# Soft mixture and rotary step: one product split over two engines, one maximum moved, one step spread over three engines

## The reference

```python
logits = einsum('bmd,dnp->bmnp', x, phi)        # 16 batches, 256 tokens, 64 x 32 slots
D = softmax(logits, over the batches)
C = softmax(logits, over all slots)
slots = einsum('bmd,bmnp->bnpd', x, D)
y = einsum('bmnp,bnpd->bmd', C, slots @ W + b)
```

```python
q, k = rms_norm(q), rms_norm(k)                 # over the 8 values of a head
q, k = apply_rope(q, cos, sin) * q_gain, apply_rope(k, cos, sin)
k = repeat(k, 4, heads)
```

## Time and profile before

| what | us |
|---|---|
| median of three runs | 3475.13 |
| lowest and highest | 3470.81, 3478.71 |
| the profiled execution, its own time | 3474.84 |
| its span in the trace | 3473.0 |
| TensorE busy in the span | 2850.8 (82%) |
| VectorE busy | 2255.4 (65%) |
| ScalarE busy | 1846.9 (53%) |
| GpSimd busy | 473.9 (14%) |
| chain that ended last | TensorE 54%, VectorE 33%, ScalarE 9% |

### The profile page before, as it was taken

How to read it: one execution, slowest core, us unless ns; L and a number is a source line. 1 busy time by engine, 2 the same in 40 slices (tenths; PEclk the granted TensorE clock), 3 DMA queues, 4 the chain that set the end, 5 groups by cost and what they waited for, 6 DMA issues and landing times.

```text
span 3473.0 us, 75794 instructions
## 1 busy us (share of the span) xinstructions
PE 2850.8 (82%) x31896; PEld 2280.3 (66%) x31896; DVE 2255.4 (65%) x5958; ACT 1846.9 (53%) x4107; POOL 473.9 (14%) x535
## 2 busy tenths in 40 slices
PE   5788887788888578788886889988888899686895
PEld 3566665556666477777775767866767688575474
DVE  4766656676666588888896754466575644754527
ACT  3566665566666477777774444354544434443332
POOL 1211101210001232222221011110000211002000
PEclk8899999999999889998998899997999999797897
DMA  2000000000000000000001000010010000001000
GB/s 94 1 2 2 1 2 1 1 2 1 14 2 14 28 7 7 7 7 7 7 1 61 3 2 25 2 50 2 17 36 3 25 2 26 26 3 49 0 1 25
DMA packets 16996, 48.95 MB, mean 14 GB/s; under 512 B 1168, under 2 KB 9616, under 8 KB 14096
## 3 DMA queue, kind: packets, MB, share of 16 engines
q1 hardware_dynamic: 16656, 44.10, 3.7%
HBM read 41.99 MB, written 2.10 MB: 13 GB/s over the span
## 4 chain that ended last, share of the span: by engine, by line
PE 54%; DVE 33%; ACT 9%; issue 2%; POOL 1%; DMA 0%; DVEq 0%; SPq 0%; POOLq 0%; ACTq 0%
PE ps L329 7%; DVE LN L2048 5%; PE ps L320 5%; PE ps L1926 3%; PE ps L1357 3%; PE ps L386 3%; PE ps L473 3%; DVE M L489 2%; DVE RS L239 2%; DVE LN L2061 2%; PE ps L1368 2%; PE ps L294 2%; PE ps L1870 2%; PE ps L754 2%; ACT LN L302 1%
## 5 line engine op out<-in xcount | busy, mean ns | idle before, releaser
L302 ACT COPY LN<-ps 128x512 f32<-128x512 f32 (+4 forms) x560 | 286.3, 550 | 277.5 <-PE ps L294 55.2
L281 POOL TENSOR_TENSOR RS<-RS,MISC 128x4 f32<-128x4 f32 x184 | 189.1, 1028 | 1462.7 <-DVE RS L263 781.1
L489 DVE TENSOR_REDUCE M<-ps 128x6 f32<-128x768 f32 x256 | 241.4, 954 | 135.3 <-PE ps L473 94.7
L294 PE MATMUL ps<-cons,LN 128*128 128x128 f32 x672 | 122.0, 318 | 164.2 <-ACT LN L268 57.0
L2048 DVE TENSOR_TENSOR LN<-LN 128x1024 f32<-128x1024 f32 (+2 forms) x192 | 220.3, 1147 | 27.0 <-ACT LN L302 16.1
L386 PE MATMUL ps<-LN 32*128 32x256 f32 x1024 | 187.9, 440 | 54.9 <-DVE LN L525 31.5
L294 PEld LDWEIGHTS ps<-cons,LN 128*128 128x128 f32 x672 | 88.3, 162 | 206.0 <-ACT LN L268 54.3
L320 PE MATMUL ps<-LN,wAB 128*128 128x512 f32 x384 | 202.6, 660 | 19.4 <-DVE LN L959 18.0
L1926 PE MATMUL ps<-LN,wAB 128*128 128x128 f32 x1024 | 151.2, 310 | 74.9 <-ACT LN L302 74.4
L633 DVE TENSOR_REDUCE M<-ps 128x12 f32<-128x1536 f32 x64 | 112.4, 1756 | 147.8 <-PE ps L376 147.8
L389 PE MATMUL ps<-LN 32*128 32x256 f32 x1024 | 202.0, 473 | 2.4 <-DVE M L489 2.4
(11 more groups left out here) (361 smaller groups left out, 7367.2 us busy)
## 6 DMA issues: line engine op xcount, KB each, us to landing
LN<-frame SPq DMA_DIRECT2D x16, 1024.0 KB, 5.1
wAB<-wb SPq DMA_DIRECT2D x16, 256.0 KB, 2.6
LN<-frame SPq DMA_DIRECT2D x8, 512.0 KB, 3.5
LN<-wd SPq DMA_DIRECT2D x8, 512.0 KB, 6.9
wAB<-wa SPq DMA_DIRECT2D x1, 3840.0 KB, 17.0
wCs<-wc SPq DMA_DIRECT2D x1, 2336.0 KB, 8.8
XA<-xin SPq DMA_DIRECT2D x8, 256.0 KB, 8.3
y<-XA SPq DMA_DIRECT2D x8, 256.0 KB, 2.3
```

What stands on the lines that cost most here:

```text
L281: pool.e.tensor_tensor(c.r[:, 40:44], c.r[:, 36:40], mhalf, ALU.pow).then_inc(*c.G.inc((k, "rstd")))
L294: ins = pe.e.transpose(ps[:, n * 128:(n + 1) * 128], src[:, n, :], ident)
L302: act.e.copy(dst, ps).then_inc(*c.A.inc(named(k, done)))
L489: return dve.e.tensor_reduce(cols[:, 2 - 2 * h:4 - 2 * h, :, q.at], src, X_AX, ALU.max, negate=True)
```

## The change

It has four parts.

1. In the soft mixture GpSimd's product for the first tile is shared: VectorE multiplies batches 0 to 7 (1024 columns, new L2091, straight behind its reciprocal), GpSimd batches 8 to 15. The second tile's product stays whole on GpSimd. TensorE waits for both halves.
2. For the second tile the maximum over the slots and the small steps behind it come ahead of the batch tree and the subtraction; for the first tile the order stays.
3. In the rotary step ScalarE takes the square (it does so right behind its copies), and the scale and epsilon go into ScalarE's root, with epsilon as a column in SBUF that is written at the program's start.
4. The four copies of the key heads go from VectorE to GpSimd; TensorE transposes the queries first and waits for GpSimd only before the keys.

```diff
@@ pe_mid
             pe.wait_ge(c.D, (k, "roped"))
             pe_tr4(pe, c, k, v["QK"][:, :, 0:128], 0, c.D, "qa")
+            pe.wait_ge(c.G, (k, "repeated"))
             pe_tr4(pe, c, k, v["KR"], 1, c.A, "ka")
@@ dve_mid
-            dve.wait_ge(c.A, (k, 1, "qkv"))
-            dve.e.tensor_tensor(sq, QK, QK, ALU.mult).then_inc(*c.D.inc())
-            dve.wait_ge(c.D)
-            dve.e.tensor_reduce(rb, sq.rearrange("p t (h d) -> p (t h) d", d=8), X_AX, ALU.add).then_inc(*c.D.inc())
-            dve.wait_ge(c.D)
-            dve.e.tensor_scalar(rb, rb, 0.125, EPS, ALU.mult, ALU.add).then_inc(*c.D.inc((k, "ms")))
+            dve.wait_ge(c.A, (k, "qk_sq"))
+            dve.e.tensor_reduce(rb, sq.rearrange("p t (h d) -> p (t h) d", d=8), X_AX, ALU.add).then_inc(*c.D.inc((k, "ms")))
...
-            dve.e.tensor_tensor(QK, sq, un, ALU.add).then_inc(*c.D.inc())
-            dve.wait_ge(c.D)
-            for t in range(4):
-                kr4 = v["KR"][:, t, :].rearrange("p (g r d) -> p g r d", g=4, d=8)
-                k3_ = QK[:, t, 128:160].rearrange("p (g d) -> p g d", d=8)
-                ins = dve.e.tensor_copy(kr4, k3_.unsqueeze(2).to_broadcast([128, 4, 4, 8]))
-            ins.then_inc(*c.D.inc((k, "roped")))
+            dve.e.tensor_tensor(QK, sq, un, ALU.add).then_inc(*c.D.inc((k, "roped")))
@@ act_mid
+            act.wait_ge(c.A, (k, 1, "qkv"))
+            act.e.activation(v["sq"], QK, ACT.Square).then_inc(*c.A.inc((k, "qk_sq")))
             yield
             act.wait_ge(c.D, (k, "ms"))
-            act.e.activation(v["rb"], v["rb"], ACT.Sqrt).then_inc(*c.A.inc((k, "rms")))
+            act.e.activation(v["rb"], v["rb"], ACT.Sqrt, scale=0.125, bias=epsc).then_inc(*c.A.inc((k, "rms")))
@@ pool_mid
-            yield from idle(5)
+            yield from idle(3)
+            pool.wait_ge(c.D, (k, "roped"))
+            for t in range(4):
...
+                ins = pool.e.tensor_copy(kr4, k3_.unsqueeze(2).to_broadcast([128, 4, 4, 8]))
+            ins.then_inc(*c.G.inc((k, "repeated")))
+            yield from idle(2)
@@ pe_slots
+                if mt == 0:
+                    pe.wait_ge(c.D, (k, "disp"))
                 pe.wait_ge(c.G, (k, mt, "disp"))
@@ dve_front
+        def dve_minus_batch_max(dve, c, k, mt, v):
+            dve_over_batches(dve, c, v["L3"], v["D3"], v["m1"], ALU.max)
+            dve.wait_ge(c.D)
+            dve.e.tensor_tensor(v["D3"], v["L3"], v["mb"], ALU.subtract).then_inc(*c.D.inc((k, mt, "D")))
...
-            dve_over_batches(dve, c, v["L3"], v["D3"], m1, ALU.max)
-            dve.wait_ge(c.D)
-            dve.e.tensor_tensor(v["D3"], v["L3"], v["mb"], ALU.subtract).then_inc(*c.D.inc((k, mt, "D")))
+            if mt == 0:
+                dve_minus_batch_max(dve, c, k, mt, v)
             dve.e.tensor_reduce(tm, v["L3"], X_AX, ALU.max).then_inc(*c.D.inc())
...
             dve.e.tensor_scalar(v["nm"], tm, -1.0, None, ALU.mult).then_inc(*c.D.inc((k, mt, "nm")))
+            if mt == 1:
+                dve_minus_batch_max(dve, c, k, mt, v)
@@ dve_weights
             dve.e.reciprocal(v["m1"], v["m1"]).then_inc(*c.D.inc((k, mt, "m1")))
+            if mt == 0:
+                dve.wait_ge(c.D, (k, mt, "m1"))
+                dve.e.tensor_tensor(v["D3"][:, 0:8, :], v["D3"][:, 0:8, :], v["mb"][:, 0:8, :],
+                                    ALU.mult).then_inc(*c.D.inc((k, "disp")))
@@ pool_half
-                pool.e.tensor_tensor(v["D3"], v["D3"], v["mb"], ALU.mult).then_inc(*c.G.inc((k, mt, "disp")))
+                b0 = 0 if mt else 8
+                pool.e.tensor_tensor(v["D3"][:, b0:16, :], v["D3"][:, b0:16, :], v["mb"][:, b0:16, :], ALU.mult).then_inc(
+                    *c.G.inc((k, mt, "disp")))
@@ dve_program
+            dve.e.memset(epsc, EPS).then_inc(*DD[LANES].inc("epsc"))
```

More of the change, by code:

```diff
@@ L205, in build @@
         XG = [XA[:, 4 * g:4 * g + 4, :] for g in range(8)]
-        mhalf, mone = MISC[:, 0:4], MISC[:, 212:216]
+        mhalf, mone, epsc = MISC[:, 0:4], MISC[:, 212:216], MISC[:, 216:217]
         WI_S = wCs[:, 0:1152].bitcast(I32)
@@ L1761, in pool_mid @@
             pool_mean_square(pool, c, k, mhalf)
-            yield from idle(5)
+            yield from idle(3)
+            pool.wait_ge(c.D, (k, "roped"))
+            for t in range(4):
+                kr4 = v["KR"][:, t, :].rearrange("p (g r d) -> p g r d", g=4, d=8)
+                k3_ = v["QK"][:, t, 128:160].rearrange("p (g d) -> p g d", d=8)
+                ins = pool.e.tensor_copy(kr4, k3_.unsqueeze(2).to_broadcast([128, 4, 4, 8]))
+            ins.then_inc(*c.G.inc((k, "repeated")))
+            yield from idle(2)
         def pool_fold(pool):
@@ L2051, in dve_over_batches @@
             dve.e.tensor_tensor(out_, src[:, 0, :], src[:, 1, :], op).then_inc(*c.D.inc())
+        def dve_minus_batch_max(dve, c, k, mt, v):
+            dve_over_batches(dve, c, v["L3"], v["D3"], v["m1"], ALU.max)
+            dve.wait_ge(c.D)
+            dve.e.tensor_tensor(v["D3"], v["L3"], v["mb"], ALU.subtract).then_inc(*c.D.inc((k, mt, "D")))
         def dve_front(dve, c, other, q, mt):
             k, before, v = ("smoe", q), ("smoe", q - 1), views2(c, mt)
-            tm, al, mr, m1 = v["tm"], v["al"], MR[:, mt, :], v["m1"]
+            tm, al, mr = v["tm"], v["al"], MR[:, mt, :]
             dve.wait_ge(c.A, (k, mt, "L", 3))
```

## The result

| kernel | median (us) | lowest, highest (us) | runs |
|---|---|---|---|
| before | 3477.76 | 3470.69, 3485.96 | 9 |
| with the change | 3461.41 | 3451.95, 3469.07 | 9 |

The ratio is **0.9957**, 95% interval 0.9945 to 0.9969: the change takes 0.43% off, some 15 us. (The two medians in the table lie 16 us apart.) The profiled execution took 3462.27 us (span 3460.4), against 3474.84 (3473.0) before. The forecast was 3460.

What follows compares the result with a forecast made beforehand. No engine is full; a chain through several engines bounds the soft mixture, VectorE's lanes the rotary stretch. 3474.84 - 8.8 (soft mixture) - 6.4 (rotary) = 3459.6, so a median of 3460 us, range 3450 to 3471.

Steps and rivals of the forecast that it cites:

- Who gets in first: Soft mixture: VectorE's shared product L2091 starts some 0.04 us ahead of GpSimd's product and takes its undisturbed 1.22 us.
- The rival: Soft mixture: L2091 starts behind GpSimd's product and waits, 2.2 us later, program 3498; chance 0.09 together with a waiting reduction.
- The reduction is undisturbed under GpSimd: Soft mixture: the second tile's slot maximum starts 1.17 us behind the reciprocal and takes 2.28 beside GpSimd's product.
- r to e of 9.28, -4.8 in 16 halves: Soft mixture: first tile's reciprocal to second tile's exponential falls from 9.59 to 9.28 us, 0.3 less a half.
- The clock, -4 over the stage: Soft mixture: earlier TensorE restarts meet less low clock in halves 10 to 15; 0 to 18 us possible, -4 taken.
- The rotary step, -6.4: Rotary stretches, two in phase 3: lanes save 3.0 us and the tail 0.2, so -3.2 a stage.

Runs made afterwards that it cites:

- late start: The whole change plus one small VectorE step between the first tile's reciprocal and its shared product: 3491.02 us, ratio 1.0044 to the kernel before.
- mixture part alone: The kernel before with only the soft mixture changed (product shared, second tile's maximum moved): 3466.8 us, ratio 0.9981.
- a bit slower: The kernel before with two small idle VectorE steps ahead of the second tile's subtraction: 3479.47 us, ratio 1.0015.
- maximum moved: The kernel before with only the second tile's maximum over slots moved ahead of its tree, GpSimd keeping the whole product: 3481.24 us, ratio 1.003.
- rotary part alone: The kernel before with only the rotary step spread (ScalarE's square and root, GpSimd's copies): 3465.77 us, ratio 0.9976.
- deferred one: The kernel before with the rotary changes, and both GpSimd products started only behind the second tile's reciprocal: 3378.48 us, ratio 0.9719.

## Why the prediction was right, by its steps

- **Who gets in first.** Right, and the step on which all hung: L2091 started 0.034 us behind the reciprocal in all sixteen halves, and GpSimd 0.08 behind it (0.17 in half 0). The rival was real: its price was given as 2.2 us a half and 3498 for the program, and the late start showed 2.25 and 3491. The Trainium skill (SBUF — State Buffer, Who interferes with whom) says that issue order decides who blocks; both half 0 and half 11 of the late start agree.
- **The reduction is undisturbed under GpSimd.** Right: start 1.18 behind the reciprocal (1.17 said), 2.28 us long.
- **r to e of 9.28, -4.8 in 16 halves.** Right: 9.28 to 9.30 in halves 1 to 15, over all 16 halves together -4.5. But what the step priced as one thing was two: sharing gives 1.15 us a half and the moved maximum takes 0.86 back. The rows for this were at hand; the prediction never priced the parts apart, and so did not see that one of them loses.
- **The clock, -4 over the stage.** The term that failed in size. The six late halves gave 6.1 us, of which 1.7 are the linear gain, so -4.4 as forecast, and they are no longer 41.0 apart. But halves 1 to 9 took 335.88 us instead of 335.02, although each has 0.28 less work ahead of its exponential: some 3 us came back there, with the low level lasting 68.7 us instead of 65.3. The mixture gave -6.6 and not -8.8; what is left for the clock is -2.1. That it is the clock is read from its low level going up and down with these times; no run held the clock fixed. The step also weighed the clock by TensorE's idleness ahead of the restart, and that does not decide it (see "The clock"). The step looked at the six halves with a pattern in them and took the others to be neutral. With a scatter of 1 to 2 us between equal stages the size of the give-back is not well known, and the kernel with the mixture part alone, the same code, gave 8.6 us in the mixture, which would have made the term right. The sign of what came back is better known: three kernels (this, a bit slower, maximum moved) paid more in halves 1 to 9 than their work alone asks.
- **The rotary step, -6.4.** -7.3: the lanes as said on average (-3.2 a stage for -3.0; they are 6.40, 7.63 and 6.82 us apart in one stage, 6.82, 7.20 and 6.82 in the other, so two lie outside the 6.8 to 7.4 of the prediction), and GpSimd's four copies at 1.00 us instead of the 1.4 taken, which put L389 at 2.17 instead of 2.45 behind the sum. ScalarE's square (0.74 us) is hidden. The remark on "offloading operations between those two" (the Trainium skill, Perfetto Trace Analysis, Optimizing Scalar/DVE Operations) did not hold for the copies here, nor for the product: the share of it that went from GpSimd to VectorE took 27 us off the mixture.
- **The rest.** +1.3 us outside both places. It is the balance of four stretches with hardly any changed code, and these differ by more than that from one trace to the next, so nothing of it can be put down to the change.

The mixture gave 2.2 less than forecast, the rotary step 0.9 more, and the rest added 1.3: from the sum, 3459.6, that leads to 3462.2, and the profiled execution took 3462.27. The mechanism was right; that the forecast of 3460 lies within 2 us of the median, 3461.41, is in part luck, since the runs of this kernel spread over 17 us and two terms missed in opposite directions.

## What to carry to other kernels

Where an engine's instruction is much longer than the same instruction undisturbed, ask first whether the other engine's work could run at another time: here one changed wait was worth over five times the whole change (0.9719 against 0.9976 with the rotary part alone), because it moved GpSimd's product to where VectorE reads PSUM. Filling a wait with useful work gains only if that work is due before what the chain waits for; price each part of such a reordering by the time to the instruction that the next engine waits for (here the exponential), not by the engine's busy time. And where two engines are released by the same signal, the order of their starts is a number to defend: 0.04 us carried this change, and one more small step on the wrong side costs 30.

The best kernel here is the deferred one with the rotary part, 3378 us, 2.8% under the kernel before. In its later halves VectorE is busy for 32.09 of 33.70 us, so there VectorE's own work is likely the next bound; TensorE, with 30.74 us, is not far behind, and no run tried it.

## What the runs showed of the hardware

- Engines meet not only at semaphores, as the opening of this document has it: in the late start VectorE's product waits for a semaphore of its own only, and is held by GpSimd's all the same. A start 0.01 us ahead decides for VectorE: 1.23 us against 3.36 for the same instruction. The one that is held shows the wait inside its own duration, and its recorded start is the same as if it ran.
- The width of the instruction does not protect it: a step of 16 columns with two SBUF operands was 2.49 us long behind GpSimd's product (0.17 undisturbed), a reduction of 2048 columns with one SBUF operand was not held at all.
- Four GpSimd copies of 128 columns, in runs of 8, take 1.00 us together. GpSimd's product of 1024 columns takes 2.36 and that of 2048 columns 4.55. VectorE does the 2048 in 2.29.
- The late halves stayed 41.0 us apart for three amounts of work within 0.7 us of each other, and left that value when the exponential came 0.3 us earlier.
- Behind 1.40 and 3.39 us of idleness TensorE restarted at full clock, behind 5.50 and 5.79 at half, but behind 3.00 at half as well. Between halves of equal work, 3.4 us more at the low level went with 1.3 us.
